# Expert feed-forward with blocks of two and three token tiles: tiles divided per expert, next weights split inside one block

## The reference, cut to what matters

```python
CAPACITY_FACTOR = 1.25
C = max(1, math.ceil(CAPACITY_FACTOR * T / E))        # T = 20000, E = 8: C = 3125
logits = x @ gate_w + gate_b
probs = softmax(logits); idx = argmax(probs); prb = probs[idx]
pos = (cumsum(one_hot, axis=0) * one_hot).sum(-1) - 1   # rank of the token in its expert
kept = pos < C
buf = zeros((E, C, D)).at[idx, pos_safe].set(x, mode='drop')
hmid = relu(einsum('ecd,edf->ecf', buf, w1) + b1)       # D = 256, F = 1024
ybuf = einsum('ecf,efd->ecd', hmid, w2) + b2
y = nan_to_num(ybuf[idx, pos] * (prb * kept))
```

## Time and profile before

| | us |
|---|---|
| median of 3 runs | 1626.28 (1623.14 to 1627.87) |
| the profiled execution | 1618.4 |
| its span, first to last instruction | 1616.6 |
| PE busy in the span | 1333.6 (82%) |
| DVE, ACT, POOL busy | 1001.7, 975.3, 1003.8 |
| expert blocks, from the first `up` to the last `y_sum` | 662.3 to 1595.7 |

### The profile page before, as it was taken

One profiled execution on the slowest core, in us unless ns is written; L12 is line 12 of the kernel. 1 busy time (PEld: TensorE's weight loads), 2 busy tenths in 40 slices (PEclk: granted clock), 3 DMA queues, 4 the chain that ended last, 5 costly groups with the idle time before them and its releaser, 6 DMA issues.

```text
span 1616.6 us, 27019 instructions
## 1 busy us (share of the span) xinstructions
PE 1333.6 (82%) x8165; PEld 1145.9 (71%) x8167; DVE 1001.7 (62%) x2035; ACT 975.3 (60%) x2044; POOL 1003.8 (62%) x901
## 2 busy tenths in 40 slices
PE   2336699882299377699999999999999999999994
PEld 0223355552156144699998999999999999998994
DVE  7779689991299886355645545555555565455553
ACT  4877877771166422476656666665666566665663
POOL 6884777765466200666665766676566667665665
PEclk9966778997599689799999999999999999999997
DMA  9898554444676000342242422243332223222423
GB/s 334 279 331 276 183 74 67 66 61 53 155 239 220 16 9 1 91 96 41 41 98 40 95 45 42 43 95 46 77 57 40 45 56 82 45 42 37 95 43 43
DMA packets 131663, 153.38 MB, mean 95 GB/s; under 512 B 16784, under 2 KB 118352, under 8 KB 131472
## 3 DMA queue, kind: packets, MB, share of 16 engines
q0 software_dynamic: 50112, 62.49, 23.8%
q1 hardware_dynamic: 58784, 67.60, 12.9%
q10 hardware_dynamic: 22704, 22.63, 4.2%
HBM read 100.18 MB, written 52.49 MB: 94 GB/s over the span
## 4 chain that ended last, share of the span: by engine, by line
PE 55%; issue 2%; POOL 1%; ACT 1%; DVE 0%; DMA 0%; ACTq 0%; POOLq 0%; DVEq 0%
PE f_ps_y L1439 27%; PE f_ps_h L1427 25%; PE f_ps_x L1417 2%; PE f_ps_y L1458 1%; POOL out L1316 0%; POOL xg L1303 0%; POOL sg L1307 0%; DVE y_sum L1526 0%; DMA out<-clean,put_now 0%; ACT y_all L1375 0%; ACT h_all L1365 0%; DMA sg<-stat_rows,idx_now 0%; ACT f_xn L1349 0%; ACTq L1278 0%; ACTq L1277 0%
## 5 line engine op out<-in xcount | busy, mean ns | idle before, releaser
L1303 POOL DMA_INDIRECT xg<-out,idx_now x156 | 192.0, 1231 | 336.0 <-issue 228.6
L1439 PE MATMUL f_ps_y<-w_hi,h_hi 128*128 128x256 f32 x1200 | 346.9, 289 | 0.0
L1439 PE MATMUL f_ps_y<-w_hi,h_lo 128*128 128x256 f32 x1200 | 337.6, 281 | 0.0
L1439 PE MATMUL f_ps_y<-w_lo,h_hi 128*128 128x256 f32 x1200 | 337.5, 281 | 0.0
L1427 PE MATMUL f_ps_h<-x_hi,w_hi 128*128 128x384 f32 x800 | 274.1, 343 | 12.0 <-ACT h_all L1365 8.3
L1316 POOL DMA_INDIRECT out<-clean,put_now x153 | 247.1, 1615 | 52.3 <-issue 46.8
L1427 PE MATMUL f_ps_h<-x_lo,w_hi 128*128 128x384 f32 x800 | 272.5, 341 | 0.0
L1427 PE MATMUL f_ps_h<-x_hi,w_lo 128*128 128x384 f32 x800 | 272.3, 340 | 0.0
L1364 ACT ACTIVATE h_hi<-f_ps_h,c_b 128x384 fp32r<-128x384 f32 x400 | 239.6, 599 | 31.8 <-issue 14.4
L1375 ACT ACTIVATE y_all<-y_sum,prob 128x256 f32<-128x256 f32 x150 | 65.4, 499 | 303.3 <-DVE y_sum L1526 303.3
L1365 ACT ACTIVATE h_all<-f_ps_h,c_b 128x384 f32<-128x384 f32 x400 | 241.0, 602 | 0.0
(11 more groups left out here) (194 smaller groups left out, 2485.2 us busy)
## 6 DMA issues: line engine op xcount, KB each, us to landing
xin<-in_x SPq DMA_DIRECT2D x40, 512.0 KB, 5.7
out<-xin ACTq DMA_DIRECT2D x40, 512.0 KB, 4.6
rows<-out SPq DMA_DIRECT2D x38, 512.0 KB, 4.1
w_raw<-in_w SPq DMA_DIRECT2D x18, 1024.0 KB, 5.1
dst_row<-in_dst SPq DMA_DIRECT2D x20, 256.0 KB, 3.7
xg<-out,idx_now POOLq DMA_INDIRECT x156
sg<-stat_rows,idx_now POOLq DMA_INDIRECT x156
out<-clean,put_now POOLq DMA_INDIRECT x153, 3.8
```

Source lines behind the costliest of these rows:

```text
L1303: nc.gpsimd.indirect_dma_start(xg[:, i, :], None, out, bass.IndirectOffsetOnAxis(idx_now[:, i, 0:1].bitcast(U32), 0), bounds_check=ROWS - ...
L1439: ins = nc.tensor.matmul(ps_y[:, i], x[:, f, i * P:(i + 1) * P], weights[s][:, w], start=i == 2 and f == 0 and n == 0, stop=f == KF - 1 an ...
```

## The change

Each expert now gets exactly the tiles that it needs, at least 8 (9 are made 10). With t tiles it gets t // 3 + 1 blocks; 3 (t // 3 + 1) - t of them, the first ones, are **narrow**: they use two of their three tiles. The rest are **wide**. `first_wide` holds where an expert's wide blocks begin. For the counts above:

| expert | 0 | 1 | 2 | 3 | 4 | 5 | 6 | 7 | sum |
|---|---|---|---|---|---|---|---|---|---|
| blocks before | 6 | 5 | 9 | 5 | 9 | 9 | 4 | 3 | 50 |
| tiles after | 17 | 14 | 25 | 14 | 25 | 25 | 12 | 10 | 142 |
| blocks after | 6 | 5 | 9 | 5 | 9 | 9 | 5 | 4 | 52 |
| of these narrow | 1 | 1 | 2 | 1 | 2 | 2 | 3 | 2 | 14 |

In a narrow block `up`, the ReLUs and `split_hidden` take 256 columns instead of 384, `down`, `y_sum` and `y_all` two tiles instead of three. The gathers, the normalisation, the transposes, `x_hi`, `x_lo`, the tests for infinities, `clean` and the adding of rows still take three tiles. The next expert's weights are split in the first wide block alone, a cut with every slice. The routing stage gets the additional arithmetic.

```diff
-EB = -(-CAP // BR)
+ET = -(-CAP // P)
+EB = ET // BT + 1
+LEAST_TILES = 8
...
-            chain.mark(ts(blocks[:], blocks_sum[:], float(LEAST), None, ALU.max))
+            chain.mark(ts(tiles_least[:], tiles_sum[:], float(LEAST_TILES), None, ALU.max))
...
+            chain.mark(stt(out=tiles[:], in0=tiles_least[:], scalar=9.0, in1=tiles_least[:], op0=ALU.is_equal,
+                           op1=ALU.add))
...
+            chain.mark(ts(tiles_43[:], tiles[:], 43.0, None, ALU.mult))
+            chain.mark(ts(tiles_third[:], tiles_43[:], 7, None, ALU.logical_shift_right))
+            chain.mark(ts(blocks[:], tiles_third[:], 1.0, None, ALU.add))
+            chain.mark(stt(out=narrow[:], in0=blocks[:], scalar=float(BT), in1=tiles[:], op0=ALU.mult, op1=ALU.subtract))
...
+            chain.mark(tt(first_wide[:], begin[:1], narrow[:1], ALU.add))
...
+            chain.mark(tt(skipped[:], half_i[:], own_narrow[:], ALU.min))
+            chain.link(stt(out=begin_tile[:], in0=own_block[:], scalar=float(BT), in1=high_i[:], op0=ALU.mult, op1=ALU.add))
+            tt(slot_tile[:], begin_tile[:], skipped[:], ALU.add).then_inc(slots_ready, 1)
...
         def bounds(engine, e):
             return (engine.value_load(first_block[0:1, bass.ds(e, 1)], min_val=0, max_val=NB - LEAST),
+                    engine.value_load(first_wide[0:1, bass.ds(e, 1)], min_val=1, max_val=NB - LEAST + 1),
                     engine.value_load(first_block[0:1, bass.ds(e + 1, 1)], min_val=LEAST, max_val=NB))
...
-                    start, end = bounds(act, e)
-                    step(e, start, (1 - s, 0))
-                    step(e, start + 1, (1 - s, 1))
-                    with act.Fori(start + 2, end) as b:
-                        step(e, b)
+                    start, wide, end = bounds(act, e)
+                    with act.Fori(start, wide) as b:
+                        step(e, b, 2)
+                    step(e, wide, BT, 1 - s)
+                    with act.Fori(wide + 1, end) as b:
+                        step(e, b, BT)
...
+                    start, wide, end = bounds(pe, e)
+                    with pe.Fori(start, wide) as b:
+                        step(e, b, s, 2)
+                    with pe.Fori(wide, end) as b:
+                        step(e, b, s, BT)
...
                 for j in range(KJ):
-                    split_hidden(b, j)
+                    split_hidden(b, j, n)
                     if split is not None:
-                        s, half = split
-                        weights.split_low(v, tt, e + 1, s, half * KJ + j)
+                        weights.split_low(v, tt, e + 1, split, 2 * j)
+                        weights.split_low(v, tt, e + 1, split, 2 * j + 1)
                     if j == 0:
                         add_infinities(b - 1)
                     if j == 1:
                         keep_finite(b - 1)
```

More of the change, by code:

```diff
@@ L1086, in _ @@
             chain.wait(1)
-            chain.mark(red(blocks_sum[:], more[:], AX.X, ALU.add))
+            chain.mark(red(tiles_sum[:], more[:], AX.X, ALU.add))
             chain.wait(1)
@@ L1327, in _ @@
             gather(1)
-            blocks = bounds(pool, NEXP - 1)[1]
+            blocks = last_bound(pool)
             with pool.Fori(0, blocks) as b:
@@ L1395, in step @@
                         keep_prob()
-                    if split is not None and f % 2:
-                        s, half = split
-                        weights.split_high(nc, act, e + 1, s, half * KJ + f // 2)
+                    if split is not None:
+                        weights.split_high(nc, act, e + 1, split, f)
                 take_high(b + 1)
-                scale_rows(b)
+                scale_rows(b, n)
             with act.Fori(0, NEXP // 2) as pair:
@@ L1430, in up, with down @@
                 ins.then_inc(h_ready, 1)
-            def down(b, s, j):
+            def down(b, s, j, tiles):
                 pe.wait_ge(h_taken, KF * b + (2 * j + 2 + SLOTS))
                 pe.wait_ge(h_lo_ready, KJ * b + (j + 3))
-                for i in range(BT):
+                for i in range(tiles):
                     for f in (2 * j, 2 * j + 1):
@@ L1442, in down, with step @@
                 return ins
+            def step(e, b, s, tiles):
+                pe.wait_ge(hi_ready, CUTS * e + CUTS)
+                pe.wait_ge(lo_ready, CUTS * e + CUTS)
+                pe.wait_ge(x_hi_ready, b + 1)
+                pe.wait_ge(x_lo_ready, b + 1)
+                for f in range(KF):
+                    up(b, s, f, tiles)
+                pe.wait_ge(y_sum_ready, b + 1)
+                nc.tensor.matmul(ps_y[:, :2].rearrange("p i c -> p (i c)"), zero_row[:, :P], zero_row[:],
+                                 start=True, stop=False)
+                for j in range(KJ):
+                    ins = down(b, s, j, tiles)
+                    if j == 0:
+                        turn(b + 1)
+                ins.then_inc(y_ready, 1)
             turn(0)
@@ L1531, in _ @@
                     e = 2 * pair + s
-                    start, end = bounds(v, e)
-                    step(e, start, (1 - s, 0))
-                    step(e, start + 1, (1 - s, 1))
-                    with v.Fori(start + 2, end) as b:
-                        step(e, b)
-            blocks = bounds(v, NEXP - 1)[1]
+                    start, wide, end = bounds(v, e)
+                    with v.Fori(start, wide) as b:
+                        step(e, b, 2)
+                    step(e, wide, BT, 1 - s)
+                    with v.Fori(wide + 1, end) as b:
+                        step(e, b, BT)
+            blocks = last_bound(v)
             find_infinite(blocks - 1)
```

115 lines of the change are left out of this document (60 added, 55 removed).

## The result

The changed kernel takes 1646.55 us (median of 4 runs, 1638.41 to 1647.28), the kernel before 1625.38 us beside it (4 runs): a ratio of 1.0118, 95% interval 1.0088 to 1.0148. It is slower by 1.2%, and the prediction was 1647 us.

What follows compares the result with a forecast made beforehand. PE bounds the kernel, with the round 1.9 us behind. Stage 8.3, clock 8.0, third bound 2.4 and routing 2.0 make +20.7: profiled 1618.4 to 1639.1, median 7.9 above, so 1647 us; range 1621 to 1668.

Steps and rivals of the forecast that it cites:

- The bound: Expert stage: PE is never idle in a block; the round through four engines has 1.9 us slack against two blocks.
- N N: Two narrow blocks in a row: PE idle 5.1 us before h_lo in the second, both over at 31.9 us.
- N's first block: First narrow block behind a wide one: loses 1.3 us waiting for h_lo and takes 14.0 us.
- N W: A narrow block followed by a wide one: 35.2 us against 36.5, so 1.3 of 5.6 us spared.
- The split: All eight weight cuts in one block: nothing counted; up to 2 us in eight blocks if ACT's cover is gone.
- The clock: PE's clock falls behind the idleness of two narrow blocks in a row: five times 1.6, 8.0 us.
- Pair starts: The jump back to the next expert pair, where ACT stands for 4.30 us, stays as it is.
- The small terms: A third bound loaded per expert on PE, ACT and DVE, 2.4 us; additional routing-chain operations, 2.0 us.
- PE's share: A narrow block alone on PE takes 12.65 us instead of 18.25, with up matmuls 0.121 us apart.
- A: Expert stage: PE decides alone, POOL finishing an iteration in under 12.7 us; 1589 us, chance 0.09.
- B: The round holds but is shorter, POOL's iteration 13.1 us; 1626 us if the clock doesn't fall either; chance 0.13.
- C: Code: passing from narrow to wide loop costs an engine about 4 us, 32 us in all; 1679 us, chance 0.08.

Runs made afterwards that it cites:

- e4: Kernel before with DVE's wait for written rows, put_now, clean and keep_finite moved two pairs later: 1620.57 us, ratio 0.9978 to the kernel before.
- e1: Changed kernel with DVE's wait for written rows, put_now, clean and keep_finite moved two pairs later: 1616.4 us, ratio 0.9944 to the kernel before.
- f3: Changed kernel with POOL gathering (from the third block on) and adding only two tiles per block, third chip: 1594.07 us, ratio 0.9797 to the kernel before.
- e3: Kernel before with all eight weight cuts in the expert's first block: 1630.72 us, ratio 1.0031 to the kernel before.
- f1: The changed kernel run again, unaltered, on the third chip: 1645.57 us, ratio 1.0122 to the kernel before.
- f2: The same kernel as e1 run again on the third chip: 1614.97 us, ratio 0.9933 to the kernel before.
- f4: e1 plus a hint at the pair loop's jump back on PE, ACT and DVE, third chip: 1606.82 us, ratio 0.9877 to the kernel before.
- e7: e1 with ACT's eight weight cuts moved behind x_hi and DVE's behind x_lo, second chip: 1658.0 us, ratio 0.988 to the kernel before.
- e9: e7 plus the jump-back hint at the pair loop, second chip: 1641.46 us, ratio 0.982 to the kernel before.
- e5: The same kernel as f3 on the second chip: 1640.39 us, ratio 0.9808 to the kernel before.

## Why the prediction was right, point by point

- **The number.** 1647 against 1646.55 is closer than the terms deserve. Between the profiled executions +20.7 was forecast and +20.0 came; stage and routing together make +18.9 of it, where the terms say 20.7. Several terms below are off by 2 to 10 us, in both directions, and cancel. What the experiments bear out is the mechanism, not half a microsecond.
- **The bound.** "The round has 1.9 us of slack against two blocks of PE": shown by e4 (the later wait changes nothing in the stage before) and e1 (it takes 27 us from the changed one). That POOL's three tiles are what is long in it: shown by f3.
- **N N.** Forecast 5.1 us of idleness before `h_lo` and `put_now` 11.5 to 12 us into the block; 5.07 and 11.86 came. The block was to take about 18 us and took 20.88: the lost clock costs 2.6 and not 1.6, and PE alone needs 12.90 and not 12.65. This holds for one pair of five. In the others PE stood for 2.04 to 3.90 us, and the term "five times 5.1 us" is too large by 10 us.
- **N's first block.** 14.0 forecast, 14.78 measured, for the wrong reason: f3 has it without a late round, and there 1.4 us of its excess are issue at the start of the loop and the wait for ACT.
- **N W.** 35.2 forecast; 14.76 + 21.78 = 36.5 measured, so it gives nothing against two blocks of 18.25. Of the 1.3 us too much 0.8 lie in the narrow block and 0.6 in the wide one.
- **The split.** "Nothing" is a step that failed. e3 prices it at 7.3 us for the whole stage, near 1 us an expert, where the bound of 2 us an expert was put in the range and 0 in the sum. Its reason (ACT paces `up`) was not the cover that the prediction named. That price is from wide blocks; what of it is paid behind a late round was not measured apart, and N W leaves room for 0.6 us.
- **The clock.** Forecast 8.0 us. From the granted clock in windows of 4 us, half of the time at the lower level counted as lost, the stage of the change loses 13.7 us behind its first 8 and that of before 3.4: +10.3. Six stretches fell: three pair starts and the N N of experts 4, 5 and 7. Before, two of the pair starts had fallen. In f1 it is 18.9 us in nine stretches, the N W of experts 1 and 3 among them, which the prediction had counted as nothing.
- **Pair starts.** "Stays as it is" was wrong in its effect. The stand of ACT and the late round are not added: PE stands for ACT by 3.7 to 4.0 us there, and for `h_lo` in the second block by 2.0 to 2.1 instead of expert 5's 5.1. While ACT stands, POOL catches up. Experts 2, 4 and 6 came out at -1.5, -4.8 and +11.2, against -2.7, -2.7 and +14.3. It works against the split, the expert starts and the dearer clock, and is, as I read it, why the sum is closer (+16.9 against +18.7) than its terms.
- **The small terms.** Routing 2.0 forecast, 1.95 measured. The third bound was put at 0.3 each, 2.4 in all, and came out larger: PE's waits named issue at expert starts are 0.72 to 0.75 us where before none showed, and 1.25 to 1.28 at pair starts against 0.50 to 0.53. In sum 6.7 against 1.5 us, +5.2, above the bound of 4.8. Whether the load or the second loop is the cause was not tried.
- **PE's share.** A narrow block on PE alone 12.65 forecast, 12.90 measured. `up` with 256 columns: 0.119 us from start to start, at the lower bound that the prediction had, and 0.121 taken. The estimate drawn there from the figures of the Trainium skill, "TensorE: Matmul & The Clock Gate", section "Back-to-back issue gap", 17 ns saved, would have given 0.161; the measurement decides against it.
- **Rivals.** A (PE alone decides, 1589): f3 shows that this is what the kernel does when POOL has a third less to do, 1594 us. B (POOL's DMAs shorter): no, 14.90 us. C (code between the loops): no; from the narrow to the wide loop PE shows no issue wait. `issue` before `h_hi` is 14.4 us in three waits, all at the jumps back; before, the same three made 12.4, so they grew by 2.0.

## What to carry to other kernels

When work is cut on the busiest engine, compare the length of the whole round behind it with the new block, not with the old one: here 1.9 us of slack turned into up to 5 us of idleness because two narrow blocks are 11 us shorter and POOL's part of the round was left at three tiles. Then look at where in the order the wait stands: the same work with the wait two pairs later went from 1.2% slower to 0.6% faster, with two lines changed. And a saving that comes with more blocks must pay for them: experts 6 and 7, with a block more each, lost 26 us where the other six together gained 9.

## What the runs showed of the hardware that I had not expected

- **Now and then a POOL gather is held until DVE's unbroken work ends.** In the changed kernel it happened in the split block, without the cuts being moved. POOL and DVE:

```profile
912.31 1.10 POOL L1341 DMA_INDIRECT sg<-stat_rows,idx_now  x1 [0.31 <-issue]
913.71 5.39 POOL L1337 DMA_INDIRECT xg<-out,idx_now  x1 [0.30 <-issue]
919.41 1.01 POOL L1341 DMA_INDIRECT sg<-stat_rows,idx_now  x1 [0.30 <-issue]
```

```profile
911.82 1.28 DVE L1235 TENSOR_TENSOR w_lo<-w_raw,w_hi 128x512 fp32r<-128x512 f32 x2
...
918.11 0.97 DVE L1511 TENSOR_TENSOR x_lo<-f_ps_x,x_hi 128x768 fp32r<-128x768 f32 x1
919.68 0.96 DVE L1566 TENSOR_TENSOR y_sum<-f_ps_y,b 128x768 f32<-128x768 f32 x1 [0.60 <-PE f_ps_y L1473]
```

  The gather begins at 913.71 and ends at 919.10; DVE's run ends at 919.08. It came in five split blocks of the profiled execution and in four of f1; with the wait two pairs later (e1, f2, f4) no POOL DMA of the stage takes over 3 us, and none does in the kernel before or in e3. Long DVE work alone is not the condition. This run of DVE's had begun at 909.95, and two DMAs of POOL's passed within it, in 1.09 and 1.10 us. In e1 sixteen began with over 5 us of unbroken DVE work ahead and took 1.23 to 1.45 us; there one such run of DVE's goes from 912.49 to 920.48:

```profile
913.49 1.44 POOL L1337 DMA_INDIRECT xg<-out,idx_now  x1 [0.30 <-issue]
915.24 1.23 POOL L1341 DMA_INDIRECT sg<-stat_rows,idx_now  x1 [0.30 <-issue]
```

  All 25 long DMAs of the changed kernel, f1, e7 and e9 ended within 0.03 us of the end of DVE's run. What picks the one that is held stays open. In expert 2 the late round then meets the load of the next weights, and the block at 940 takes 20.24 us instead of 18.3; but expert 5 has a block of 20.00 with no held gather, where POOL's add stands for 3.75 us during such a load.
- **The lower clock lasted longer behind a stand of 5.07 us than I had read from one of 2.94:** 5.9 us of matmuls at a spacing of 0.213, against some 3.3. The length of the stand does not decide alone whether the clock falls: it fell behind 2.05 us (expert 4) and, in f1, behind 2.22 and 2.23, and not behind 2.10 and 2.12 (experts 6 and 1) or, in the kernel before, 2.57.
- **One of three chips was 3% off in all its runs** (1670.8 against 1625.6 and 1627.2 us for the same kernel), with waits on it that the others don't show; whether it is so at other times was not seen. For the kernel of e5 and f3 the ratios on two chips agreed (0.9808 and 0.9797), while the lengths of its narrow blocks did not (16.4 and 12.9 us); so block lengths were compared on one chip only.
